# The last tile of 106 rows in two pieces, and transposes two tiles ahead, in a graph layer with expert routing

## What is computed

```
x = x + gnn(layernorm(x), src, dst)
x = x + ffn(layernorm(x))
def gnn(x):
    agg = segment_sum(x[src], dst)                  # rows gathered along 106250 edges
    h = x @ W_self + b_self + (agg / degree) @ W_neigh
    h = layernorm(h) * gamma + beta
    return where(h >= 0, h, alpha * h) + x
def ffn(x):                                         # 16 experts, top 2 of each row
    logits = x @ gate_weight.T;  top 2, softmax
    h_mean[e] = mean over e's rows of silu(x @ w1[e].T)
    y_mean[e] = h_mean[e] @ w2[e].T
    return sum over the two picks of weight * y_mean[expert]
```

## Time and profile before

| what | value |
|---|---|
| median of 3 runs | 1616.33 us (1616.28 to 1617.91) |
| the profiled execution's own time | 1613.05 us |
| its span, first to last instruction | 1610.9 us |
| busy: PE, DVE, ACT, POOL | 1167.9, 1078.0, 894.4, 984.4 us |
| chain that ended last, by engine | PE 42%, POOL 22%, issue 16%, DMA 9%, DVE 4%, ACT 3% |
| mean granted clock of TensorE | 0.895 |

### The profile page before, as it was taken

How to read it: one execution, slowest core, us unless ns; L and a number is a source line. 1 busy time by engine, 2 the same in 40 slices (tenths; PEclk the granted TensorE clock), 3 DMA queues, 4 the chain that set the end, 5 groups by cost and what they waited for, 6 DMA issues and landing times.

```text
span 1610.9 us, 36408 instructions
## 1 busy us (share of the span) xinstructions
PE 1167.9 (72%) x7640; PEld 629.2 (39%) x7648; DVE 1078.0 (67%) x2594; ACT 894.4 (56%) x1939; POOL 984.4 (61%) x1254
## 2 busy tenths in 40 slices
PE   4989899999666555655556565676666339999975
PEld 2545444444322222222222222234444226676741
DVE  6776326666677576777878777656657975777626
ACT  3455455555645444444445544437666787788810
POOL 6223177676777777777777777777777006766400
PEclk9999999999979788889978878879999759999975
DMA  6445278877888888888888889888888527777548
GB/s 208 144 146 170 84 229 276 266 232 253 271 277 276 269 253 248 258 290 293 303 294 298 297 270 302 253 242 252 251 248 243 212 87 234 244 234 238 145 168 299
DMA packets 140572, 384.92 MB, mean 239 GB/s; under 512 B 22286, under 2 KB 22416, under 8 KB 140452
## 3 DMA queue, kind: packets, MB, share of 16 engines
q0 software_dynamic: 76416, 250.05, 51.6%
q1 hardware_dynamic: 63508, 132.49, 22.9%
q10 hardware_dynamic: 528, 1.05, 0.2%
HBM read 323.78 MB, written 59.72 MB: 238 GB/s over the span
## 4 chain that ended last, share of the span: by engine, by line
PE 42%; POOL 22%; issue 16%; DMA 9%; DVE 4%; ACT 3%; POOLq 2%; DVEq 0%; SPq 0%; ACTq 0%
POOL work L642 22%; PE ps L912 14%; PE ps L1013 12%; DMA work<-table,work 7%; PE ps L1106 6%; PE ps L1117 3%; PE ps L1108 3%; POOLq L637 2%; ACT slots L827 1%; ACT wparts L817 1%; DMA work<-in_x 1%; PE ps L958 1%; PE ps L1179 1%; PE ps L1153 1%; DVE slots L1650 1%
## 5 line engine op out<-in xcount | busy, mean ns | idle before, releaser
L642 POOL DMA_INDIRECT work<-table,work x832 | 792.6, 953 | 290.6 <-issue 235.3
L1013 PE MATMUL ps<-work 128*128 x2056 | 560.8, 423 | 329.2 <-DMA work<-table,work 314.2
L1013 PEld LDWEIGHTS ps<-work 128*128 128x128 f16 x2056 | 213.7, 104 | 566.4 <-issue 416.6
L770 ACT ACTIVATE work<-work,ones 128x512 f16<-128x512 f16 x259 | 185.4, 716 | 300.4 <-PE ps L1016 300.0
L764 ACT ACTIVATE work<-iota_row,work 128x128 f16<-128x128 f32 x1040 | 331.3, 390 | 31.6 <-ACT work L770 23.9
L912 PE MATMUL ps<-wparts,slots 128*128 128x512 f16 x1176 | 273.0, 383 | 17.9 <-DVE slots L1300 11.8
L701 POOL DMA_INDIRECT slots<-x_d,betab x114 | 110.0, 965 | 139.5 <-DVE betab L1580 70.9
L912 PEld LDWEIGHTS ps<-wparts,slots 128*128 128x128 f16 x1176 | 112.1, 99 | 140.1 <-DVE slots L1300 14.3
L1382 DVE TENSOR_SCALAR inv<-ps 128x1 f32 (+2 forms) x49 | 7.8, 158 | 233.3 <-PE ps L1016 227.5
L1106 PE MATMUL ps<-work,wparts 128*128 x456 | 155.3, 381 | 0.9 <-ACT wparts L856 0.3
L856 ACT COPY wparts<-ps 128x1024 f16<-128x1024 f16 x114 | 115.2, 1011 | 38.6 <-PE ps L1117 37.4
(11 more groups left out here) (281 smaller groups left out, 1536.5 us busy)
## 6 DMA issues: line engine op xcount, KB each, us to landing
work<-in_x SPq DMA_DIRECT2D x96, 256.0 KB, 2.9
work<-in_w_t SPq DMA_DIRECT2D x48, 512.0 KB, 4.2
work<-table,work POOLq DMA_INDIRECT x832
table<-work SPq DMA_DIRECT2D x48, 256.0 KB, 2.0
x_d<-work SPq DMA_DIRECT2D x48, 256.0 KB
x_d<-slots SPq DMA_DIRECT2D x48, 256.0 KB
slots<-x_d SPq DMA_DIRECT2D x48, 256.0 KB
out_x<-slots SPq DMA_DIRECT2D x48, 256.0 KB
```

The lines of the kernel that those rows point to most:

```text
L642: pool.indirect_dma_start(out=gath[:, g % GRING, w, :], out_offset=None, in_=table[:, :], in_offset=bass.IndirectOffsetOnAxis(ap=idx_all[: ...
L770: act.activation(hot[:, slot, :, :], away[:, slot % 2, :, :], ACT.Relu, bias=ones[:, 0:1], scale=-1.0).then_inc(c_hot, 1)
L1013: pe.matmul(ps[:, ds(bank, 1), :], hot[:, s, w, :], gath_row[:, ds(at + (2 * w + half) * D, D)].unsqueeze(1), start=False, stop=True, skip ...
```

## The change

1. **Pieces.** The 106 rows of the last tile are stored to the table, loaded back from HBM and stored to the output as two DMAs, of rows 0 to 95 and of the last 10. The counts that others wait for grow by one DMA. The load of the 106 rows of x, the load of x in `gnn`, and the stores of the tile's intermediate rows (`store_x1`, `store_x2`) stay whole.
2. **Two tiles ahead.** In the table stage the transposes, the copies of their result and `normal` stand one tile further ahead of `project`. They use three PSUM banks in turn (0, 1, 7). The lists that used bank 7 move to bank 6, the edge product uses two banks twice, and DVE's `distances` is cut in halves at positions 10 and 13.
3. **Early position product.** The first `place` writes bank 6 in place of bank 5, no longer waits for `d_xt`, and stands one step earlier. ACT leaves out the distances and one-hots of steps that don't exist. `LOW_FIRST` grows from 16 to 22: so many of ACT's pairs stand ahead of the last `take_turned`. SP's waits are lowered to fit.

```
-LOW_FIRST = 16
+LOW_FIRST = 22
-POS_AT = (5, 0)
+POS_AT = (6, 0)
+EVEN = TAIL - TAIL % 16
+PIECES = ((0, EVEN), (EVEN, TAIL - EVEN))
+def pieces_of(rows):
+    return PIECES if rows == TAIL else ((0, rows),)
+        XBANKS, ZBANK = (0, 1, 7), 2
 # SP: store_table; load_x1 and store_out alike
-                sp.dma_start(table[i * P:i * P + r, :], tb[0:r, i % HALF, :]).then_inc(a_st[i % HALF], 16)
+                for a, n in pieces_of(r):
+                    sp.dma_start(table[i * P + a:i * P + a + n, :], tb[a:a + n, i % HALF, :]).then_inc(a_st[i % HALF], 16)
 # ACT, table stage
+            turned_high(0)
+            normal(2)
             for i in range(TILES):
-                if i == TILES - LIST_TILES:
+                if i + 1 == TILES - LIST_TILES:
                     act.wait_ge(b_done, 1)
-                turned_high(i)
-                if i + 2 < TILES:
-                    normal(i + 2)
+                if i + 1 < TILES:
+                    turned_high(i + 1)
+                if i + 3 < TILES:
+                    normal(i + 3)
                 if i:
                     neigh_high(i - 1)
 # ACT, steps
-                    act.wait_ge(c_hot, k + 2)
-                    distance(k + 3, (s + 3) % 2)
-                    one_hots(k + 2, (s + 2) % HOTS)
+                    if not late or k + 3 < STEPS:
+                        act.wait_ge(c_hot, k + 2)
+                        distance(k + 3, (s + 3) % 2)
+                    if not late or k + 2 < STEPS:
+                        one_hots(k + 2, (s + 2) % HOTS)
 # PE, table stage
             turn_x(0)
+            turn_x(1)
             for i in range(TILES):
-                if i + 1 < TILES:
-                    turn_x(i + 1)
+                if i + 2 < TILES:
+                    turn_x(i + 2)
                 project(i)
 # PE, steps
-                    if late and k == STEPS - 2:
-                        pe.wait_ge(d_xt, k - LATE)
+                    if late and k == STEPS - 3:
                         place(0)
 # DVE, table stage
+            turned_low(0)
             for i in range(TILES):
-                turned_low(i)
+                if i + 1 < TILES:
+                    turned_low(i + 1)
```

More of the change, by code:

```diff
@@ L324, in build @@
         a_stat, a_xs, a_t, a_hi, a_lo, a_mm, a_zhi, a_z = [sem(f"a_{n}") for n in ("stat", "xs", "t", "hi", "lo", "mm", "zhi", "z")]
-        b_cmp, b_cnt, b_later, b_jb, b_hit, b_fin, b_idx, b_rel, b_row, b_done = [
-            sem(f"b_{n}") for n in ("cmp", "cnt", "later", "jb", "hit", "fin", "idx", "rel", "row", "done")]
+        b_cmp, b_cnt, b_later, b_jb, b_hit, b_fin, b_idx, b_rel, b_row, b_done, b_half = [
+            sem(f"b_{n}") for n in ("cmp", "cnt", "later", "jb", "hit", "fin", "idx", "rel", "row", "done", "half")]
         w_max, w_tr, w_diag, w_bc, w_scale, w_hi, w_lo = [sem(f"w_{n}") for n in
@@ L480, in _ @@
             for b in range(HALF):
-                sp.wait_ge(a_st[b], 16 * len(range(b, TILES, HALF)))
+                sp.wait_ge(a_st[b], 16 * (len(range(b, TILES, HALF)) + (b == 0)))
             load_res(0, 0)
@@ L512, in load_x1 @@
             def load_x1(i, rows):
-                sp.dma_start(slots[0:rows, ds(i, 1), :], x1_d[ds(i * P, rows), :].unsqueeze(1)).then_inc(f_back, 16)
+                for a, n in pieces_of(rows):
+                    sp.dma_start(slots[a:a + n, ds(i, 1), :], x1_d[ds(i * P + a, n), :].unsqueeze(1)).then_inc(f_back, 16)
             def load_w2(e):
@@ L546, in store_out @@
                     sp.wait_ge(g_x, ready(i))
-                    sp.dma_start(out[ds(i * P, rows), :], slots[0:rows, ds(i, 1), :]).then_inc(g_out, 16)
+                    for a, m in pieces_of(rows):
+                        sp.dma_start(out[ds(i * P + a, m), :], slots[a:a + m, ds(i, 1), :]).then_inc(g_out, 16)
             rounds(sp, store_out)
-            sp.wait_ge(g_out, 16 * TILES)
+            sp.wait_ge(g_out, 16 * (TILES + 1))
         @block.gpsimd
@@ L629, in _ @@
             for b in range(HALF):
-                pool.wait_ge(a_st[b], 16 * len(range(b, TILES, HALF)))
+                pool.wait_ge(a_st[b], 16 * (len(range(b, TILES, HALF)) + (b == 0)))
             pool.wait_ge(b_done, 1)
@@ L726, in turned_high @@
                     act.wait_ge(a_mm, i - HALF + 1)
-                act.copy(xt[:, i, 0, :, 0:r], ps[:, i % 2, :].rearrange("p (c n) -> p c n", c=CHUNKS)[:, :, 0:r]
+                act.copy(xt[:, i, 0, :, 0:r], ps[:, XBANKS[i % 3], :].rearrange("p (c n) -> p c n", c=CHUNKS)[:, :, 0:r]
                          ).then_inc(a_hi, 1)
@@ L759, in _ @@
             for b in range(HALF):
-                act.wait_ge(a_st[b], 16 * len(range(b, TILES, HALF)))
+                act.wait_ge(a_st[b], 16 * (len(range(b, TILES, HALF)) + (b == 0)))
             def distance(k, par):
@@ L930, in tiles_of_steps @@
                 pe.wait_ge(b_later, 1)
-                pe.matmul(ps[:, 7, 0:STEPS], ones[0:NJ, :], later[0:NJ, :], start=True, stop=True).then_inc(b_jb, 1)
+                pe.matmul(ps[:, 6, 0:STEPS], ones[0:NJ, :], later[0:NJ, :], start=True, stop=True).then_inc(b_jb, 1)
             def edges_of_steps(lo, hi):
                 pe.wait_ge(b_hit, 1)
+                if lo:
+                    pe.wait_ge(b_half, 1)
                 for w in range(lo, hi):
                     for c in range(GROUP_CHUNKS):
-                        last = pe.matmul(ps[:, 4 + w, 0:STEPS], dstf[:, c, w * P:(w + 1) * P], hit[:, c, :],
+                        last = pe.matmul(ps[:, 4 + w % 2, 0:STEPS], dstf[:, c, w * P:(w + 1) * P], hit[:, c, :],
                                          start=c == 0, stop=c == GROUP_CHUNKS - 1)
@@ L1251, in hits @@
                 dve.wait_ge(b_jb, 1)
-                ln.link(dve.tensor_copy(jall[:, :], ps[:, 7, 0:STEPS]))
+                ln.link(dve.tensor_copy(jall[:, :], ps[:, 6, 0:STEPS]))
                 ln.link(dve.tensor_tensor(tall[:, :], kvals[:, :], jall[:, :], ALU.subtract))
@@ L1264, in step_rows, with distances @@
                 dve.scalar_tensor_tensor(steprow[0:1, :], clip[0:1, :], float(TILE_FIELD), jall[0:1, :], ALU.mult, ALU.add)
[L1266 to L1271 removed]
+            def distances(half):
+                if half == 0:
+                    dve.memset(negd[:, STEPS * GT:(STEPS + 3) * GT], 0.0)
+                dve.wait_ge(b_rel, half + 1)
+                dve.scalar_tensor_tensor(negd[:, 0:STEPS * GT].rearrange("p (k w) -> p w k", w=GT)[:, 2 * half:2 * half + 2, :],
+                                         jall[:, :].unsqueeze(1).to_broadcast([P, 2, STEPS]), float(P),
+                                         ps[:, 4:6, 0:STEPS], ALU.mult, ALU.subtract).then_inc(b_fin if half else b_half, 1)
             def end_rows():
@@ L1278, in _ @@
             lists = {LIST_AT[0] - 1: passed_tiles, LIST_AT[1] - 1: turns, LIST_AT[2] - 2: hits, LIST_AT[2] - 1: step_rows,
-                     LIST_AT[3] - 1: distances, LIST_AT[3] + 1: end_rows}
+                     LIST_AT[2]: lambda: distances(0), LIST_AT[3] - 1: lambda: distances(1), LIST_AT[3] + 1: end_rows}
             def stats_of(i):
```

32 lines of the change are left out of this document (13 added, 19 removed).

## The result

The changed kernel takes 1599.81 us (median of 4, 1598.32 to 1601.21), the kernel before beside it 1616.3 (4 runs, 1614.97 to 1617.91). The ratio is 0.9897, 95% interval 0.9884 to 0.991. The forecast was 1601.2 in 1597.0 to 1606.5. The profiled execution took 1598.56 us (span 1596.4), 14.5 less than before's.

A forecast was written before the change was run, and what follows sets the result against it. PE's waits in the table stage, POOL's gathers, ACT at the gather stage's end and the final stores were taken to bound the kernel; 3.6 + 4.1 + 3.4 + 4.0 = 15.1 us off 1616.33 gives 1601.2, range 1597.0 to 1606.5.

The forecast's parts named there:

- Pieces: Last tile's 106-row store in 96 and 10 rows: lands 4.1 us sooner at the table, 4.0 at the output.
- The 24 products at the higher level: PE's products after the table's last store may run at the higher clock, 1.9 us sooner; counted as nothing.
- Table stage: Transposes two tiles ahead remove PE's waits for low halves; 3.6 us won net, bounds -1.4 to 8.
- the pause of 2.65 us: New PE pause at the table stage's start, until tile 4's transposes, before `project(2)` at 32.85.
- two more waits: Table stage's start: PE waits 0.4 us for `passed_tiles` and 0.7 for `neigh_low(1)` behind it.
- The first rival: Table stage's start costs what the lists give back, by clock fall or late POOL chain: gain 11.5, 1604.8 us; chance 0.14.
- Slack of 1.6 us in each quad: Later table-stage quads: `neigh_high` runs 0.4 late, but PE's result is there 1.6 us early, so no cost.
- the slower rival: POOL's chain ahead of `neigh_high` decides every quad; kernel 3.2 us slower, 1620 us; chance 0.03.
- Head start through the gather stage: A gather stage starting earlier by t ends earlier by t, keeping 3.6 + 4.1 us; rival, lost there, chance 0.05.
- End of the gather stage: ACT's pairs end 3.4 us sooner, DVE's tables at 1316.1, PE at 1317.6; gain 3.4, bounds 2.5 to 3.8.
- The sum: Table stage 3.6, table landing 4.1, gather stage's end 3.4, output landing 4.0: 15.1 us in all.
- landings in turn: Rival: the two pieces land one after the other, winning 2.2 twice instead of 8.1; 1605.1 us; chance 0.06.

The follow-up runs named there:

- The run that made ACT and DVE end together: Changed kernel with two more tiles' low pairs moved from DVE to ACT at the gather stage's end: 1601.48 us against 1599.08.
- the new order at the start: Changed kernel with ACT taking the first projection's high half before scaling tile 4, PE projecting tile 2 before tile 4's transposes: 1596.21 us against 1598.44.

## Why the prediction was right, point by point

- **Pieces.** Right in mechanism and size: 4.2 and 4.4 us for 4.1 and 4.0, and 9.8 (7.8 to 12.1) for 8.1 as a part alone. The halves of 53 rows show that the number of engines does it.
- **The 24 products at the higher level** came (5.35 instead of 7.36) and gave nothing that the end shows: the gathers' head start at the end of their stage was 6.9, not more than at its beginning.
- **Table stage.** Forecast 3.6, seen 3.2. The waits for `turned_low` went and the two new pauses stood where they were put, 0.5 us off. The forecast held the clock constant across the pause of 2.65 us, and it fell there, for 1.2 us. By luck this cost little: the forecast had two more waits behind it, 0.4 for `passed_tiles` and 0.7 for `neigh_low(1)`, and PE, still at the slower products, did not meet them. Projection 3 starts at 38.89, 3.5 us behind the kernel before (35.37), where the forecast had 3. That is the 0.5 by which POOL's chain made projection 2 late. The first rival had the fall of the clock right; its price (all 3.6 lost) was too high.
- **Slack of 1.6 us in each quad** held: in later quads `normal` waits 0.8 to 4.0 us for POOL, and no pause of PE answers to it, so the slower rival was not at work.
- **Head start through the gather stage.** It kept 6.9 of 7.4 us. Its length from first to last gather varies between executions by more than that (1052.6 to 1056.6 us over fourteen traces, one of each run), which is most of the spread.
- **End of the gather stage.** Forecast 3.4, seen 2.9, alone 4.7 (2.9 to 6.5). The forecast had ACT's pairs end at 1313.4 and DVE's tables at 1316.1, and PE end at the same time by either path: with 42 products (4.15) behind ACT, or with 14 (1.4) behind DVE. ACT did end 2.9 us ahead of DVE (1307.40 against 1310.30). The step that failed is the batch behind ACT: PE did 14 products there (28 in one of three traces) and the rest behind DVE's tables, so only DVE's path was left. On it the terms differ from the forecast's: DVE's last table was to come 0.5 sooner, but it came 6.3 us earlier where the gathers ran 6.9 ahead, so 0.65 later when counted from the last gather. The products behind it took 0.91 instead of 1.4. The gain is therefore PE's: 4.47 - 0.91 = 3.56 us behind DVE's last table, less 0.65. Why DVE kept less of the head start (its `route(0)` starts 5.6 us earlier, 1227.85 against 1233.46) is not shown. The run that made ACT and DVE end together came out slower.
- **The sum.** The parts seen in the trace give 14.5 for the 15.1 forecast, with the pieces 0.5 and the expert stage 0.3 above, and the table stage 0.4, the gather stage 0.5 and its end 0.5 below: errors that in part cancel. The medians give 16.5, which the spread between executions covers. Two small slips in the forecast's arithmetic change nothing: by its own figures a fall of the clock costs 10 x 0.15 = 1.5 us, not 1.7, and landings in turn give 1604.9, not 1605.1.

## What to carry to other kernels

A partition count of a DMA is a speed: the last tile's odd rows ran on two engines of sixteen, and cutting off ten rows was worth 4 us at each of the two places where such a transfer stood alone at a stage's end; the wrong cut (53 and 53) made it worse than none. When two engines feed a third that takes its work in a fixed order, look at which of them the next piece needs: with ACT and DVE ending together PE got 42 products in one batch behind a pause of 4.2 us, at the lower clock, and with ACT 2.9 us ahead it got them piece by piece. When pricing a pause of TensorE, add the slower products behind it, and then ask which later waits they hide. Filling the pause of 2.39 us with a projection that was ready started the next one 3.3 us sooner (35.63 against 38.89).

## What the runs showed of the hardware

- **The clock after short pauses is not the same each time.** Behind PE's wait for `wpow` at 97 us (1.64 to 1.71 us in eleven traces) the next 12 products took 2.75 us in eight and 4.44 in three, in kernels whose code is the same up to there as well. Behind pauses of 1.9 to 3.2 us at 32 us they took 3.97 to 5.05 in all eight traces that have that pause, and behind 0.54 to 1.05 us (three traces) 2.75. In the three kernels with the table stage of before, 1.76 to 1.78 us at 31 us cost nothing (2.76), and neither did their pauses of 1.62 to 2.24 us at 166 us (2.76). So the length of a pause alone does not tell what the next products cost: 1.93 us at 32 us was followed by 4.43, and 2.24 us at 167 us by 2.76.
- **POOL slows beside DVE**: two instructions of 0.20 us took 0.51 to 0.72 us beside DVE's two conversions of 128 x 1024, in all six traces in which the two meet (the kernel before, the pieces alone, the end alone, and the three with the new order at the start); beside the reduction that follows them they took 0.20.
- **Two DMAs of 53 rows ran one after the other on one engine at a time** (share 0.05 to 0.08 from 188 to 198 us), though 15 of the 16 were idle.
- The halves of 53 rows gave two times, about 1613.8 and 1619; the cause stays open.
